# Expert choice in pieces between the token statistics, scatters one step later, one weighted sum ahead of a late addition

## The reference

```python
q, k, v = ln(x) @ Wq.T, ctx @ Wk.T, ctx @ Wv.T         # q and k: LayerNorm by head
attn = softmax(einsum('bhqd,bhkd->bhqk', q, k) / 8)
x = x + tanh(g_xattn) * (merge(attn @ v) @ Wu.T + bu)
h = ln(x)
logits = h @ Wg                                        # 8 experts
vals, idx = top_k(softmax(logits), 2)
weights = vals / (sum(vals) + 1e-9)
y = sum over both: weights * (silu(h @ W1[e] + b1[e]) @ W2[e] + b2[e])
shared = silu(h @ Ws1 + bs1) @ Ws2 + bs2
x = x + tanh(g_ffn) * (y + 0.1 * shared)
```

## Time and profile before

| | |
|---|---|
| runs | 600.97 us median of 3 (599.75 to 601.02) |
| profiled execution | 599.88 us, of it span 597.7 us |
| granted TensorE clock, mean | 0.991 of full speed |
| PE busy | 567.4 us (95%) |
| DVE busy | 454.2 us (76%) |
| ACT busy | 453.3 us (76%) |
| POOL busy | 359.9 us (60%) |
| attention loop | from about 20 to 396 us |
| shared groups and schedule | to about 439 us |
| expert tiles | to about 572 us |
| last sums and stores | to 597.7 us |

### The profile page before, as it was taken

One profiled execution on the slowest core, in us unless ns is written; L12 is line 12 of the kernel. 1 busy time (PEld: TensorE's weight loads), 2 busy tenths in 40 slices (PEclk: granted clock), 3 DMA queues, 4 the chain that ended last, 5 costly groups with the idle time before them and its releaser, 6 DMA issues.

```text
span 597.7 us, 21071 instructions
## 1 busy us (share of the span) xinstructions
PE 567.4 (95%) x7675; PEld 508.0 (85%) x7675; DVE 454.2 (76%) x1048; ACT 453.3 (76%) x991; POOL 359.9 (60%) x709
## 2 busy tenths in 40 slices
PE   6989999999999999999999999889989999999993
PEld 5868888888888888878888888678889999999983
DVE  4689889889898988998998899755766554555637
ACT  3689999999888999888999988666445565565574
POOL 2545656756557787777778866757716555555410
PEclk9999999999999999999999999999999999999997
DMA  6910100120100101110020000001312222222155
GB/s 216 334 42 3 36 4 21 37 83 3 54 3 13 49 25 39 43 32 11 22 64 12 21 13 10 20 29 42 125 51 77 85 74 77 86 76 65 45 223 212
DMA packets 22500, 37.07 MB, mean 62 GB/s; under 512 B 5136, under 2 KB 13072, under 8 KB 22272
## 3 DMA queue, kind: packets, MB, share of 16 engines
q1 hardware_dynamic: 17792, 26.81, 14.2%
q0 software_dynamic: 4320, 8.92, 4.2%
q10 hardware_dynamic: 288, 0.00, 0.0%
HBM read 22.71 MB, written 13.01 MB: 60 GB/s over the span
## 4 chain that ended last, share of the span: by engine, by line
PE 76%; DVE 13%; issue 5%; ACT 2%; POOL 2%; DMA 2%; ACTq 0%; DVEq 0%; SPq 0%; POOLq 0%
PE ps L1491 10%; PE ps L1237 8%; PE ps L1205 7%; PE ps L1293 7%; PE ps L1207 6%; PE ps L1206 6%; PE ps L1263 6%; PE ps L1246 5%; PE ps L1278 4%; PE ps L1475 3%; PE ps L1476 3%; PE ps L1477 3%; PE ps L1374 2%; DVE wide L847 2%; DVE sm L869 2%
## 5 line engine op out<-in xcount | busy, mean ns | idle before, releaser
L763 POOL DMA_INDIRECT results<-spo,xs_ix x71 | 69.1, 973 | 69.3 <-DVE spo L1161 59.6
L439 ACT ACTIVATE qk_T<-ps,lnw 128x512 f32<-128x512 f32 x128 | 96.9, 786 | 6.8 <-PE ps L1237 6.2
L847 DVE TENSOR_TENSOR wide<-ps,rstd 128x512 f32<-128x512 f32 x128 | 87.1, 680 | 5.0 <-POOL rstd L678 5.0
L1205 PE MATMUL ps<-w_hi,xc_hi 128*128 128x512 f32 x192 | 87.1, 454 | 3.9 <-DVE w_lo L783 2.8
L840 DVE TENSOR_REDUCE ss<-wide 128x16 f32<-128x1024 f32 x64 | 77.8, 1216 | 15.4 <-ACT wide L415 14.0
L1237 PE MATMUL ps<-ident,wide 128*128 128x128 f32 x512 | 78.4, 278 | 4.0 <-ACT row_T L491 2.5
L415 ACT ACTIVATE wide<-ps 128x512 f32<-128x512 f32 x128 | 76.1, 596 | 2.2 <-PE ps L1207 2.2
L1237 PEld LDWEIGHTS ps<-ident,wide 128*128 128x128 f32 x512 | 58.9, 144 | 20.5 <-ACT spo L469 6.5
L1207 PE MATMUL ps<-w_hi,xc_lo 128*128 128x512 f32 x192 | 76.2, 397 | 0.0
L704 POOL DMA_INDIRECT routed<-rows_all,slot x64 | 65.4, 1021 | 17.5 <-issue 16.3
L1206 PE MATMUL ps<-w_lo,xc_hi 128*128 128x512 f32 x192 | 75.6, 394 | 0.0
(11 more groups left out here) (202 smaller groups left out, 1354.3 us busy)
## 6 DMA issues: line engine op xcount, KB each, us to landing
v_sb<-routed SPq DMA_DIRECT2D x31, 130.0 KB
xc_in<-in_x SPq DMA_DIRECT2D x8, 256.0 KB, 2.9
xc_in<-in_ctx SPq DMA_DIRECT2D x8, 256.0 KB, 4.7
w_raw<-in_L_ffn_W SPq DMA_DIRECT2D x8, 256.0 KB, 2.7
out_x<-x_res SPq DMA_DIRECT2D x8, 256.0 KB, 2.0
x_res<-in_x SPq DMA_DIRECT2D x1, 1792.0 KB, 8.6
w_raw<-results SPq DMA_DIRECT2D x3, 512.0 KB, 4.6
rows_all<-results SPq DMA_DIRECT2D x3, 512.0 KB, 8.6
```

The costliest lines, as they stand in the source:

```text
L439: nc.scalar.activation(qk_T[:, n, 4 * j:4 * j + 4, :].rearrange("p a n -> p (a n)"), ps[6 + j][:, :], ACT.Identity, bias=lnw[:, 2 * n + 1: ...
L763: gp_.indirect_dma_start(out=results[:, :], out_offset=bass.IndirectOffsetOnAxis(ap=xs_ix[:, b4, a:a + 1], axis=0), in_=yb[:, b4, a, :], i ...
L847: nc.vector.tensor_tensor(qk_n[:, n, j * 512:(j + 1) * 512].rearrange("p (h d) -> p h d", h=8), ps[2 * n + j][:, :].rearrange("p (h d) -> ...
L1205: nc.tensor.matmul(out_bank, xc_hi[:, t % XD, src, :], w_hi[:, w, cols[j]], start=True, stop=False)
```

## The change

On DVE `route` is cut into single operations ("pieces"), and the helper `after` into two: `link_of`, which counts an operation, and `last`, which waits for the last one counted, now at the head of the next piece. At place 0 the first three operations stay at the end of the step (`choose_late`). The others stand in the later steps ahead of the scores' maximum, one piece before, between and behind the halves of the two statistics. So the first expert is found at place 1, the picked experts at place 2 (ahead of the maximum), slots at place 3 instead of 2. ACT takes its exponentials one place later. `SCATTER_LAG` is 16 instead of 15. Behind the loop the same operations run in the same order. At the end `combine(0)` stands ahead of `shared_out(EARLY)`.

```diff
-        SCATTER_LAG = 15
+        SCATTER_LAG = 16
...
             def route(s, lag):
                 b, at = batch_at(s, lag)
-                if b is not None and at == 0:
+                if b is not None and at == 1:
                     expert_exponentials(b)
-                if b is not None and at == 1:
+                if b is not None and at == 2:
                     second_exponentials(b)
...
-            def token_statistics(t):
+            def token_sums(t):
...
                     nc.vector.bn_stats(bn6[:, :], x_res[:, t, :]).then_inc(bn_done, 1)
+
+            def token_moments(t):
+                if has(t):
                     ve.wait_ge(bn_done, t + 1)
...
-            def after(ins):
-                choice[0] += 1
+            def last():
+                ve.wait_ge(f_step, links[0])
+
+            def link_of(ins):
+                links[0] += 1
                 ins.then_inc(f_step, 1)
-                ve.wait_ge(f_step, choice[0])
...
+            def first_choice(b):
+                last()
+                link_of(nc.vector.tensor_tensor(oh[:, 0, :, :], tie, by_expert(first_at(b)), ALU.is_equal))
...
+            def choose_late(s):
+                b, at = batch_at(s, ROUTE_LAG)
+                if b is not None and at == 0:
+                    highest(b)
+                    less_highest(b)
+                    ties(b)
+
+            def choose(s, piece):
+                b, at = batch_at(s, ROUTE_LAG)
...
+                if at == 1:
+                    if piece == 0:
+                        first_expert(b)
+                    if piece == 1:
+                        first_choice(b)
+                    if piece == 2:
+                        others(b)
+                    if piece == 3:
+                        highest_of_rest(b)
+                    if piece == 4:
+                        equal_of_rest(b)
...
                 normalise(s - 3)
-                token_statistics(s + 3)
-                second_statistics(s - 2)
+                choose(s, 0)
+                token_sums(s + 3)
+                choose(s, 1)
+                token_moments(s + 3)
+                choose(s, 2)
+                second_sums(s - 2)
+                choose(s, 3)
+                second_moments(s - 2)
+                choose(s, 4)
                 maximum(1, s)
...
                 keep_logits(s - 4)
-                route(s, ROUTE_LAG)
+                choose_late(s)
...
+            combine(0)
             shared_out(EARLY)
-            combine(0)
             combine(1)
```

More of the change, by code:

```diff
@@ L910, in first_choice, with first_expert @@
+            def first_expert(b):
+                last()
+                link_of(nc.vector.tensor_reduce(first_at(b), tie, AX.X, ALU.max))
             def first_choice(b):
[L911 to L914, removed]
+                last()
+                link_of(nc.vector.tensor_tensor(oh[:, 0, :, :], tie, by_expert(first_at(b)), ALU.is_equal))
@@ L931, in take_ranks, with hits, slots @@
                 nc.vector.tensor_tensor(base[:, b + 1, :], ps[5][:, E + BT * E:2 * E + BT * E], base[:, b, :], ALU.add).then_inc(f_taken, 1)
-            def place(b):
+            def hits(b):
                 ve.wait_ge(f_taken, 2 * b + 2)
-                after(nc.vector.tensor_tensor(hit, oh, rank.unsqueeze(1).to_broadcast([P, 2, BT, E]), ALU.mult))
+                link_of(nc.vector.tensor_tensor(hit, oh, rank.unsqueeze(1).to_broadcast([P, 2, BT, E]), ALU.mult))
+            def slots(b):
+                last()
@@ L946, in weigh, with denominator @@
[L946 to L953, removed]
+                link_of(nc.vector.tensor_reduce(gs, ge, AX.X, ALU.add))
+            def denominator(b):
+                last()
+                link_of(nc.vector.tensor_scalar(den, gs, TOPK_EPS, 1.0, ALU.mult, ALU.add))
@@ new lines, in with_second, with inverse, first_weight, second_weight @@
+            def with_second(b):
+                last()
+                ve.wait_ge(f_e1, b + 1)
+                link_of(nc.vector.tensor_tensor(den, den, e1, ALU.add))
+            def inverse(b):
+                last()
+                link_of(nc.vector.reciprocal(den, den))
+            def first_weight(b):
+                last()
+                link_of(nc.vector.tensor_scalar(wtok[:, BT * b:BT * b + BT, 0], den, tg[:, 1:2], None, ALU.mult))
+            def second_weight(b):
+                last()
+                link_of(nc.vector.tensor_tensor(wtok[:, BT * b:BT * b + BT, 1], wtok[:, BT * b:BT * b + BT, 0], e1, ALU.mult))
@@ new lines, in choose @@
+                if at == 2:
+                    if piece == 0:
+                        ties_of_rest(b)
+                    if piece == 1:
+                        second_expert(b)
+                    if piece == 2:
+                        second_choice(b)
+                    if piece == 3:
+                        both_choices(b)
+                if at == 3:
+                    if piece == 0:
+                        hits(b)
+                    if piece == 1:
+                        slots(b)
+                    if piece == 2:
+                        gate_sum(b)
+                    if piece == 3:
+                        denominator(b)
@@ L969, in route_ranks @@
+                if at == 4:
+                    if piece == 0:
+                        with_second(b)
+                    if piece == 1:
+                        inverse(b)
+                    if piece == 2:
+                        first_weight(b)
+                    if piece == 3:
+                        second_weight(b)
             def route_ranks(s, lag):
```

80 lines of the change are left out of this document (51 added, 29 removed).

## The result

| | before | after |
|---|---|---|
| median of the runs on the same chip | 601.0 us (599.75 to 602.15, 4 runs) | 596.34 us (594.41 to 596.7, 4 runs) |
| profiled execution | 599.88 us, span 597.7 us | 596.70 us, span 594.9 us |

The ratio is 0.9912, with a 95% interval of 0.9893 to 0.993: 5.3 us faster (601.0 x 0.0088). The forecast was 595.3.

What follows compares the result with a forecast made beforehand. TensorE's chain was taken to bound the kernel, with routing steps lengthened by late DVE work. 600.97 - 6.1 (loop) + 0.5 (late scatters) = 595.3 us; range 593.0 to 598.8, the forecast's own 593.8 to 596.9 (chance 0.60).

Steps and rivals of the forecast that it cites:

- The loop's gain: Three batches inside the attention loop: routing costs TensorE some 9.4 us, of which 6.1 us are gained.
- Steps 11, 19, 27: Three of six small operations stay behind the logits' copy on DVE: extra 0.76, taken as 0.28 us lost.
- Step 12: Five pieces ahead of DVE's maximum, 0.12 late; 0.5 us lost because TensorE's gap in attend loses its cover.
- Step 13: Four pieces, some 0.35, fit the idle 0.39 ahead of the maximum; the rank matmuls' 0.27 us stays.
- Steps 14 to 16 and 22 to 24: Three operations behind the logits leave in each of two steps, winning 0.6 us; 0.45 loss left per batch.
- Step 21: Attention step in batch 1: its 0.96 us loss stays, partly a TensorE gap like that in attend.
- which the 0.5 absorbs: Some 0.5 us of each routing step's extra DVE time costs TensorE nothing; assumed to cover the maximum's 0.12 lateness too.
- More is won: Rival, chance 0.12: later routing steps lose nothing, attend's gap stays covered, first expert tile not late; 593.1 us.
- Half is won: Rival, chance 0.17: each piece on DVE pays its whole 0.26 spacing, 3.5 of 6.1 won, tail takes 1.0; 598.5 us.
- The slower rival: Rival, chance 0.04: pieces on DVE hold POOL's scatters, the reciprocal root behind them comes late; 603 us.
- The scatters' lag: Behind the loop: two more scatters on POOL end 1.63 later, delaying the first expert tile; cost 0.5, bounds 0 and 1.63.
- The weighted sum: At the end: DVE starts it about a microsecond earlier, but the next late addition waits for TensorE; nothing gained.

Runs made afterwards that it cites:

- the block: Changed kernel with all pieces of a step standing together behind both statistics, still ahead of the maximum: 600.2 us, ratio 0.9972.
- filled kernel: Changed kernel with one tile's two scatters moved into POOL's idle 2.78 us ahead of the last normalised probabilities: 594.21 us, ratio 0.9883.
- the dummies: Changed kernel with 14 dummy matmuls ahead of the first row tile's transposes and 6 ahead of the second's: 595.48 us, ratio 0.9908.
- the again: Changed kernel run and profiled a second time without any edit: 596.54 us, ratio 0.9926 against the kernel before.
- kernel with the ties moved: The filled kernel with step 11's third small operation moved into step 12 and each later piece one down: 594.18 us, ratio 0.9873.
- second chip: Another chip, two runs: changed kernel with 5 and 2 dummy matmuls, 629.78 us; with 20 more at the start, 629.58; kernel before, 637.66.

## Why the prediction was right, step by step

**The loop's gain: 6.1 predicted, 6.26 measured**, and the mechanism is the one named. Spread pieces fit into the idle time ahead of the maximum, which starts at most 0.14 late against TensorE's step, and the same pieces in one block make it 0.4 to 0.6 late and cost 3.7 us. That the two numbers are so near is partly luck, since terms that were off by up to 0.8 us cancel, and the second profile has 225.70 us, a gain of 6.8. By its parts:
- Steps 11, 19, 27: 0.28 left was predicted, 0.25, 0.26 and 0.25 measured. The extra on DVE was put at 0.76 and is 0.78.
- Step 12: 0.5 for a gap whose cover goes. It left 0.57 in one profile and 0.04 in another, with and without the gap. Steps 20 and 28 were given 0.1 and left 0.16. On DVE 0.12 of lateness was predicted; it is 0.02 in step 12 and 0.13 and 0.14 in steps 20 and 28.
- Step 13: 0.27 predicted, 0.24 measured. TensorE's rank matmuls wait for nothing, though the picks are now made just ahead of the maximum of the same step.
- Steps 14 to 16 and 22 to 24: 0.45 was left in each batch, 0.05 measured. This term was too cautious: nearly all that those steps lost went with the small operations behind the logits.
- Step 21: 0.96 was predicted to stay; 1.44 was there, with a gap of 0.93 in attend. Step 29: 0.54 was to be won. In the starts of the chain it took 374.96 - 363.64 = 11.32 and takes 369.16 - 358.46 = 10.70, 0.62 won. Step 30 has a gap of 1.17 (0.98 before). The gaps of steps 21 and 30 change from execution to execution, and the one in step 21 is a good part of why the better 14 to 16 and 22 to 24 did not show in the total.

**Where its reasoning was wrong without harm.** "0.12 makes the maximum late, which the 0.5 absorbs": there is no such 0.5 for the maximum. The 0.5 belongs to work behind the logits' copy. A late maximum is paid at the logits' matmul, through the PSUM bank, and almost in full, as the block shows (0.41 to 0.57 late, 0.40 to 0.53 lost), and as steps 20 and 28 show (0.13 and 0.14 late, 0.16 lost). The spread pieces did no harm because they are hardly late. One sum of the prediction is wrong too: in the rival "More is won" the first tile is not late, so the 0.5 is not added and must not be taken off a second time; 600.97 - 6.1 - 0.9 - 0.4 is 593.6, not 593.1.

**The rival "Half is won"** (598.5, each piece pays 0.26) is what the block does: its pieces are 0.26 apart and it lands at 600.2, 1.7 above that rival's figure. Spreading is what decides between it and the forecast. **The slower rival**, pieces and scatters holding each other, did not come. POOL's 64 scatters take 65.5 us in all, 65.4 before. One row shows the sign of a shared port: step 15's tensor_scalar beside a scatter takes 0.52, and in step 23, again beside one, 0.38, where the same line takes 0.23 in step 31 and behind the loop (381.07 and 409.31).

```profile
200.99 0.96 POOL L704 DMA_INDIRECT routed<-rows_all,slot  x1 [0.30 <-issue]
...
201.41 0.52 DVE L999 TENSOR_SCALAR wtok<-w_raw,tg 128x8 f32<-128x8 f32 x1
```

The scatter beside it keeps its 0.96, and a piece with two SBUF operands beside another scatter (step 21, at 268.78) takes 0.23, where its mean over the batches is 0.248. The rule of the Trainium skill (SBUF — State Buffer, "Who interferes with whom") agrees with the tensor_scalar's two rows; no run here shows it for the others.

**The scatters' lag: 0.5 predicted, 1.9 measured.** This is the step of the sum that was mis-sized. The place was right, the first row tile's load. The scatters' end was right to a hundredth (1.63 later), but that is luck: the last scatter starts 1.26 later, and the rest is its own length of 1.33 instead of 0.96, which the sum did not have. The low part then came 0.37 late, near the 0.5. What the sum did not have is the second effect, 1.54 us of half clock behind waits of 1.60 and 0.72; with it the cost of 1.91 lies above the upper bound of 1.63. I had read the wait as time that passes once. The filled kernel takes both away, and the dummies the clock alone. The lag of 16 alone costs nothing: with waits of 0.61 and 0.61 the clock stayed.

**The weighted sum: nothing predicted, nothing measured** (23.76 with it and without), and for the reason given: the second late addition waits longer.

With the two measured terms the sum would have read 600.97 - 6.26 + 1.91 = 596.6; the median is 596.34. The forecast of 595.3 was 1 us low. Open is the 0.88 of the expert tiles: the again and the filled kernel took 124.63 and 124.35, so one execution's late row tile is likelier than the change. What was late isn't shown: the trace after names DVE's cast of weights (L1248) as what ended that wait, where the profile before names the load of a row tile.

## What to carry to other kernels

In this kernel small operations that depend on each other, in a row, cost DVE their full spacing of 0.26 us each; each beside an independent one, they cost about half of that, and five of them fitted into 0.55 us of idle time. So spread them through work that ends in a wait. Look for two prices when the first big engine's wait grows: the wait, and the clock behind it; and before paying either, look for idle time on the engine that is late (here 2.78 us on POOL took two scatters, for 2.15 us of that stretch in one profile). A lag that only postpones a consumer may be what makes an earlier producer's delay affordable; test both without each other before calling one of them a cost.

## What the runs showed of the hardware

- TensorE's granted clock fell to its lower level for most of 4 us (0.57 to 0.58 on average) behind waits of 1.60 and 0.72 us that ended 1.1 us apart. It fell in all four profiles with such a pair (the others had 1.48 and 0.67, 1.54 and 0.56, 1.69 and 0.56). It stayed at 1.00 behind 0.61 and 0.61, behind 0.28 and 1.16, and with the waits filled. But waits alone don't settle it: behind 0.94, 1.22 and 0.40 it fell in one profile (0.50 at 392 to 394 us, kernel with the ties moved) and stayed at 1.00 in four others with the same three (the changed kernel twice, the filled one, the one with 14 dummies).
- TensorE has gaps that no engine releases. In the ten profiles of the first chip they lie at six places of its program, and their length changes from execution to execution: 0.35 to 1.17 at one (step 21), 0.43 to 1.52 at another (step 30), 0 or 0.31 to 0.86 at a third (step 12). On the second chip one of about 0.4 came in every attention step from 15 on, which made most of them 11.9 us instead of 11.15. In the attention steps the matmuls around them are the shortest of the kernel (64x64), but behind the loop the second chip also has gaps of up to 2.41 us among matmuls of 128x128. What makes them isn't shown.
- A scatter of 128 rows takes 0.96 us behind the loop, but 1.33 as the last one of the changed kernel and 1.30 as the third from last of the filled one. The 0.37 moves the first row tile's load. What sets this wasn't tried.
